# The rows of v by SBUF-to-SBUF DMA from a fourfold copy instead of by matmul, gamma in the collecting weights

## The reference, cut to what matters

```
q, k, v = split(layernorm(h) @ Wqkv.T + b)      # 16 heads of 16 channels
k = k / 4
retention = 1 - sigmoid(Lambda_raw)             # per head, 16 x 16
for every token t:
    hebbian[i, j] = v_t[i] * k_t[j]
    state = retention * state + Gamma * hebbian
    y_t[i] = sum_j (W_static[i, j] + state[i, j]) * q_t[j]
out = y @ out_w.T + out_b
```

## Time and profile before

| | us |
|---|---|
| median of 3 runs | 365.59 |
| lowest, highest | 363.73, 366.17 |
| span of the profiled execution | 360.0 |
| busy: DVE, PE, POOL, ACT | 302.0, 274.5, 207.5, 183.8 |
| first scan starts, last product ends | 45.72, 334.17 |

### The profile page before, as it was taken

The page is one execution under the profiler, slowest core; times in us unless marked ns, Lnnn a source line. Parts: engine busy times, 40 slices in busy tenths (PEclk is TensorE's granted clock), DMA queues, the critical chain, the costliest instruction groups (busy, mean ns, idle before and its releaser), DMA issues. The chain is left out here.

```text
span 360.0 us, 4155 instructions
## 1 busy us (share of the span) xinstructions
PE 274.5 (76%) x1214; PEld 141.5 (39%) x1214; DVE 302.0 (84%) x443; ACT 183.8 (51%) x336; POOL 207.5 (58%) x175
## 2 busy tenths in 40 slices
PE   5786899965979777965998498559978546747792
PEld 4674225531322353632333366223324213205581
DVE  0144098999999999999999999999999999999262
ACT  3236593455654704775768037576763168610152
POOL 5777676447873913747768317547876158970010
PEclk9899995996898799896999989887996956859899
DMA  6711200000010000000111000000210000001001
GB/s 168 251 46 49 75 7 2 3 0 0 13 50 26 0 3 1 0 0 29 36 50 33 4 1 0 0 31 0 74 44 3 0 0 0 0 15 46 0 2 58
DMA packets 10502, 10.07 MB, mean 28 GB/s; under 512 B 3344, under 2 KB 8944, under 8 KB 10480
## 3 DMA queue, kind: packets, MB, share of 16 engines
q1 hardware_dynamic: 9200, 7.70, 7.1%
q0 software_dynamic: 1280, 2.11, 2.1%
HBM read 4.95 MB, written 2.10 MB: 20 GB/s over the span
## 5 line engine op out<-in xcount | busy, mean ns | idle before, releaser
L380 POOL TENSOR_TENSOR uu<-vg,kk 128x512 f32<-128x512 f32 x128 | 160.1, 1275 | 99.7 <-ACT vg L566 93.7
L566 ACT ACTIVATE vg<-vr_ps,gam_sb 128x512 f32<-128x512 f32 x128 | 83.1, 687 | 20.3 <-PE vr_ps L882 12.6
L690 DVE TENSOR_TENSOR_SCAN zz<-r_ps,uu 128x512 f32<-128x512 f32 x64 | 77.2, 1214 | 10.3 <-POOL uu L380 10.3
L690 DVE TENSOR_TENSOR_SCAN zz<-r_ps,carry,uu 128x512 f32<-128x512 f32 x64 | 79.1, 1273 | 0.0
L711 DVE TENSOR_TENSOR zz<-zz,q_ps 128x1024 f32<-128x1024 f32 x64 | 76.4, 1196 | 0.0
L882 PE MATMUL vr_ps<-v_rows,selv 96*128 96x512 bf16 x100 | 40.5, 441 | 18.3 <-ACT vg L566 18.1
L896 PE MATMUL y_ps<-zz,sely 128*32 128x512 f32 x256 | 41.0, 717 | 15.2 <-DVE zz L711 15.2
L882 PEld LDWEIGHTS vr_ps<-v_rows,selv 96*128 96x128 bf16 x100 | 9.7, 102 | 55.8 <-ACT vg L566 38.9
L352 POOL TENSOR_TENSOR tok<-tok,bf 128x1024 f32<-128x1024 f32 x4 | 9.4, 2357 | 30.9 <-ACT tmp_b L482 29.3
L423 ACT ACTIVATE tok<-scr 128x512 f32<-128x512 f32 x16 | 9.5, 591 | 24.4 <-PE scr L812 17.5
L760 PE MATMUL scr<-wexp,emb_t 128*128 128x256 f32 x64 | 20.6, 479 | 1.0 <-ACT emb_t L415 1.0
(11 more groups left out here) (95 smaller groups left out, 413.3 us busy)
## 6 DMA issues: line engine op xcount, KB each, us to landing
v_rows<-v_part SPq DMA_DIRECT2D x84, 32.0 KB, 1.9
out_h<-tok SPq DMA_DIRECT2D x8, 256.0 KB, 2.2
wexp<-in_w_exp SPq DMA_DIRECT2D x1, 256.0 KB, 2.8
tok<-in_table,ids_sb POOLq DMA_INDIRECT x16, 2.8
wproj<-in_w_proj SPq DMA_DIRECT2D x1, 256.0 KB, 5.0
wv<-in_w_v SPq DMA_DIRECT2D x1, 256.0 KB, 4.8
wk<-in_w_k SPq DMA_DIRECT2D x1, 256.0 KB, 4.9
wq<-in_w_q SPq DMA_DIRECT2D x1, 256.0 KB, 5.3
```

The lines of the kernel that those rows point to most:

```text
L380: pool.tensor_tensor(uu[:, slot % NU, :], vg[:, slot % NVG, :], kk[:, c % 2, hg, :], ALU.mult).then_inc(s_u, 1)
L566: act.activation(vg[:, slot % NVG, :], vr_ps[:, slot % NVR, :], ACT.Copy, scale=gam_sb[:, n:n + 1]).then_inc(s_vg, 1)
L690: dve.tensor_tensor_scan(zz[:, g % NZ, :], r_ps[:, n:n + 1].to_broadcast([P, T]), uu[:, g % NU, :], start, ALU.mult, ALU.add).then_inc(s_s ...
```

## The change

- The splitting of v in three parts, `spread`, the PSUM buffers `vr_ps`, and ACT's copy with gamma go. v goes to SBUF once per head group, in fp32 (`v_sb`).
- `copy_v(c)` on SP, per chunk: for each head group four DMAs of 256 KB write `v_sb` to four places of an HBM tensor `v_far`. Then for each head group SP waits for these four and issues one DMA of 1 MB that reads them back as `v_four`. In it partition (h, j4, b) holds the rows a = 0..3, so each row of v lies on four partitions.
- `row(g)` on SP, per unit: one DMA of 256 KB from 32 partitions of `v_four` (each read four times, source step 0) straight into `vg`. POOL waits for it in place of ACT. There are eight `vg` buffers as before, and the DMA for unit g waits until POOL is done with unit g-8.
- `copy_v(c+1)` stands in SP's order behind `row` of unit 29 of chunk c, `store(c-1)` behind that of unit 31.
- gamma goes in the collecting weights: `gsel = sely * gamma`, two DVE instructions at the end of the prologue (`w_gam`); PE waits for them at slot 0.
- `wake` of the last chunk now uses `q_ps` and waits for all 64 products of DVE (`s_z`) instead of ACT's last `vg`. The calendars are otherwise unchanged but for the stages removed.

```diff
-NVR, NVG, NU, NZ = 2, 8, 8, 16
+NVG, NU, NZ = 8, 8, 16
+COPY_AT = 29
...
+            def copy_v(c):
+
+                for hg in range(HG):
+                    taken(sp, "v", c, hg)
+                    for j in range(NA):
+                        sp.dma_start(v_far[HG * c + hg, :, j], v_sb[:, hg, :]).then_inc(s_vfar[hg], 16)
+                for hg in range(HG):
+                    sp.wait_ge(s_vfar[hg], 16 * NA * (c + 1))
+                    if c >= 2:
+                        sp.wait_ge(s_u, UNITS * (c - 2) + HD * (hg + 1))
+                    sp.dma_start(v_four[:, c % 2, hg], v_far[HG * c + hg].rearrange("h j b a t -> (h j b) a t"))\
+                      .then_inc(s_v4[hg], 16)
+
+            def row(g):
+
+                c, n, hg, a, b = unit(g)
+                if n % HD == 0:
+                    sp.wait_ge(s_v4[hg], 16 * (c + 1))
+                if g >= NVG:
+                    sp.wait_ge(s_u, g - NVG + 1)
+                src = v_four[b::NB, c % 2, hg, a, :].rearrange("p (o t) -> p o t", o=1)
+                sp.dma_start(vg[:, g % NVG, :], src.to_broadcast([P // NB, NB, T])).then_inc(s_vrow[g % NVG], 16)
...
-            move_v(0)
-            for c in range(1, NC):
-                if c >= 2:
-                    store(c - 2)
-                move_v(c)
-            store(NC - 2)
+            copy_v(0)
+            for g in range(NC * UNITS):
+                row(g)
+                c, n, hg, a, b = unit(g)
+                if n == COPY_AT and c + 1 < NC:
+                    copy_v(c + 1)
+                if n == UNITS - 1 and c >= 1:
+                    store(c - 1)
             store(NC - 1)
...
-                    pool.wait_ge(s_vg, slot + 1)
+                    pool.wait_ge(s_vrow[slot % NVG], 16 * (slot // NVG + 1))
...
+            def v(c, hg):
+                bank = filled(act, "v", c, hg)
+                if c >= 1:
+                    act.wait_ge(s_vfar[hg], 16 * NA * c)
+                act.activation(v_sb[:, hg, :], scr[:, bank, :], ACT.Identity, bias=bv[:, hg:hg + 1])\
+                   .then_inc(s_free[bank], 1)
...
-                    act.wait_ge(s_vr, slot + 1)
-                    if slot >= NVG:
-                        act.wait_ge(s_u, slot - NVG + 1)
-                    n = slot % UNITS
-                    act.activation(vg[:, slot % NVG, :], vr_ps[:, slot % NVR, :], ACT.Copy,
-                                   scale=gam_sb[:, n:n + 1]).then_inc(s_vg, 1)
...
+            def w_gam(*_):
+                dve.wait_ge(s_w_unit, 48)
+                for hg in range(HG):
+                    units = slice(HD * hg, HD * (hg + 1))
+                    gam_of = gam_sb[:, units].rearrange("p (b a o) -> p b a o", a=NA, o=1)
+                    dve.tensor_tensor(gsel[:, units, :].rearrange("p (b a) m -> p b a m", a=NA),
+                                      sely[:].rearrange("p b (o m) -> p b o m", o=1).to_broadcast([P, NB, NA, 32]),
+                                      gam_of.to_broadcast([P, NB, NA, 32]), ALU.mult).then_inc(s_gsel, 1)
...
-                    bank = vr_ps[:, 0, :]
-                    pe.wait_ge(s_vg, NC * UNITS)
+                    bank = q_ps[:, 0, :]
+                    pe.wait_ge(s_z, NC * UNITS // 2)
...
-                    last = pe.matmul(y_ps[32 * a:32 * a + 32, :], sely[:, b, :], zz[:, (g + a) % NZ, :],
+                    last = pe.matmul(y_ps[32 * a:32 * a + 32, :], gsel[:, n + a, :], zz[:, (g + a) % NZ, :],
                                      start=False, stop=True, skip_group_check=True)
```

More of the change, by code:

```diff
@@ L124, in tower_kernel @@
     SLOTS = range(-1, (NC + 1) * UNITS)
-    uses = [key for slot in SLOTS for key in pe_at.get(slot, []) if not key[0].startswith(("v_less", "wake"))]
+    uses = [key for slot in SLOTS for key in pe_at.get(slot, []) if not key[0].startswith(("wake",))]
     use = {key: (n % 2, n // 2) for n, key in enumerate(uses)}
@@ L190, in tower_kernel @@
         q_sb = sb("q_sb", [P, HG, T])
-        v_part = [sb(f"v_part{p}", [P, HG, T], BF16) for p in range(PARTS)]
-        v_rows = sb("v_rows", [PARTS * 32, 2, HG, NA, T], BF16)
+        v_sb = sb("v_sb", [P, HG, T])
+        v_far = nc.dram_tensor("v_far", [NC * HG, P // HD, NA, NB, NA, T], F32).ap()
+        v_four = sb("v_four", [P, 2, HG, NA, T])
         y_t = sb("y_t", [P, HG, T])
@@ L231, in tower_kernel @@
         s_cast = sem("s_cast")
[L232 removed]
+        s_gsel = sem("s_gsel")
         s_sig = sem("s_sig")
@@ L861, in _ @@
             operand = {"expand": "base_t", "corr": "masked_t", "v": "xhat_t", "k": "xhat_t", "q": "xhat_t"}
-            def spread(g):
-                c, n, hg, a, b = unit(g)
-                direct = DIRECT if c else HD
-                if n == HD or n == direct:
-                    for p in range(PARTS):
-                        pe.wait_ge(s_vrows[p][hg], 16 * NA * moves(c, hg))
-                if g >= NVR:
-                    pe.wait_ge(s_vg, g - NVR + 1)
-                if n < direct:
-                    if n == 0:
-                        taken(pe, "v", c, 0)
-                    rows_a = slice(32 * a, 32 * a + 32)
-                    for p in range(PARTS):
-                        last = pe.matmul(vr_ps[:, g % NVR, :], selv[rows_a, b, :], v_part[p][rows_a, 0, :],
-                                         start=(p == 0), stop=(p == PARTS - 1))
-                    last.then_inc(s_vr, 1)
-                    return
-                pe.matmul(vr_ps[:, g % NVR, :], selv[0:PARTS * 32, b, :], v_rows[:, c % 2, hg, a, :],
-                          start=True, stop=True).then_inc(s_vr, 1)
             def collect(g):
@@ L960 @@
         "w_k": halves(w_qkv[DIM:2 * DIM].T),
-        "w_v": halves(w_qkv[2 * DIM:][rows].T),
+        "w_v": halves(w_qkv[2 * DIM:][v_rows].T),
         "b_q": b_qkv[:DIM].reshape(HG, P).T,
         "b_k": b_qkv[DIM:2 * DIM].reshape(HG, P).T,
-        "b_v": b_qkv[2 * DIM:][rows].reshape(HG, P).T,
+        "b_v": b_qkv[2 * DIM:][v_rows].reshape(HG, P).T,
         "w_o": halves(g["L0_attn_out_w"].T[rows]),
```

137 lines of the change are left out of this document (40 added, 97 removed).

## The result

| | before | after |
|---|---|---|
| median, lowest to highest | 364.71, 363.73 to 366.17 | 399.01, 396.82 to 402.07 |
| ratio, 95% interval | | 1.0948 [1.0877, 1.1019] |
| span of the profiled execution | 360.0 | 394.9 |

A forecast was written before the change was run, and what follows sets the result against it. The prediction took DVE to bound the 128 units. First scan +6.0, boundaries +4.5, end +6.0 and DVE's short instructions -11.5 made +5.0 us: a median of 370.6 us against 365.59, range 359 to 381 us.

The forecast's parts named there:

- The first scan: Start of the units: the chain of writes, read, row and multiplication delays the first scan from 45.72 to 51.8 us, +6.0 us.
- the price of a write: Copy of v to HBM: at 340 GB/s, 256 KB take 0.77 us of the DMA engines.
- SP's issuing: Copy of v before the first scan: issuing at 0.59 us a DMA is hidden below the transfers.
- v_four much beyond 15 us: Sign named in advance: the prediction is wrong if `v_four` lands much beyond 15 us after v.
- My upper bound: First scan: each of three hops 1.4 us slower, as the slowest `v_rows` landed, +10.3 us.
- The boundaries: Between chunks: `uu` of unit 30 comes 16 us after v; just in time once, 2.9 us late at unit 62; +4.5 us.
- The end: After the last product: wakes and collections now wait for it on PE, 8.0 us less a faster projection; +6.0 us taken.
- DVE's short instructions: In the units: POOL no longer waits for ACT, so stretched chain instructions give back 9.6 us and `carry` 2; -11.5 us.
- The rule of one POOL instruction per hit: In the units: a short DVE instruction waits until the POOL instruction in flight is done, about 1.24 us.
- the release by ACT: Cause given for POOL's bursts: it waited 93.7 us for ACT's `vg`, then caught up under DVE's layernorm chain.
- At nothing: Row transfers cost nothing: 0.77 us of the engines and 0.59 of SP against 1.74 us per unit; the traffic slows nobody.
- (D): Rival, chance 0.05: rows bind if a row's DMA takes over 1.74 us; at 2.2 us a row the kernel takes 424 us.

The follow-up runs named there:

- e13: Changed kernel, but each write of v to HBM goes in 32 blocks of 8 KB instead of 8 of 32 KB: 371.0 us, before beside it 362.9.
- e1: Changed kernel, but the last wakes use their own PSUM bank and wait for POOL's last `uu`, not DVE's last product: 423.1 us, before beside it 395.3.
- e17: e13 with the last wakes on their own bank behind POOL's last `uu` instead of DVE's last product: 392.2 us, before beside it 391.3.
- e0: The changed kernel run again, nothing altered: 399.8 us, before beside it 362.9, ratio 1.1013.
- e11: Changed kernel, but POOL makes each `uu` in two multiplications of 128x256 instead of one of 128x512: 411.1 us, before beside it 362.9.
- e18: Kernel before, but POOL may be three units ahead of DVE instead of eight: 379.9 us, before beside it 392.8, ratio 0.9691.
- e8: Changed kernel, but rows come straight from a doubled `v_sb`, 8 partitions read sixteen times, no HBM copy; wakes as in e1: 416.5 us, before beside it 395.3.
- e2: Changed kernel, but v is written to HBM once per head group and copied fourfold by four reads of 256 KB: 419.1 us, before beside it 395.3.

## Why the prediction was wrong

*The first scan, forecast +6.0, measured +14.8.* The step that failed is the price of a write: 0.77 us for 256 KB, from the window in which weights load. Those loads fill 128 partitions; the writes of v go to eight blocks, and eight engines carried them at 155 GB/s, 1.7 us each, 13.5 us for the eight. So the second read was out 14.3 us behind v at the first boundary and 15.8 in the prologue, not at 7.6. The price was taken by bytes, not by shape. The 1 MB reads were priced right: 3.1 us at 340 GB/s, found 332. Hung on to it: SP's issuing, costed at nothing, took 10.3 us for the eight writes in the prologue, so the first read went out 10.4 us behind v and not at 4.5:

```profile
34.98 10.33 SPq L288 DMA_DIRECT2D v_far<-v_sb  x8
...
45.35 5.39 SPq L293 DMA_DIRECT2D v_four<-v_far  x2
...
53.64 7.37 SPq L304 DMA_DIRECT2D vg<-v_four  x9
```

The first row, which waits for the first read, went out 18.7 us behind v (34.95 us); "v_four much beyond 15 us" was a sign of being wrong that the prediction had named. My upper bound (+10.3) stretched the landings and left the rate alone, so it did not cover the case either.

*The boundaries, forecast +4.5, measured +24.7.* The same chain, three times; the multiplication of unit 30 started 20.7 us behind v and not at 14.6. (The forecast's own parts, nothing, 2.9 and 2.9 us, add up to 5.8 and not to the 4.5 taken.) Unit 30 was to be just in time and came 6.4 us late, unit 62 was to be 2.9 late and came some 9 us late. With the writes at sixteen engines (e13) `uu` of these units started 15.1 to 15.5 us behind v, and the kernel took 371.0 us, +8.1 over before on its chip. Its parts are near the forecast ones, +8.2, +7.1, +6.2 and -12.9 us where +6.0, +4.5, +6.0 and -11.5 stood: the forecast was about that of a kernel whose writes use all engines. That the medians, 371.0 and 370.6 us, all but meet is luck, since before took 362.9 us there and not 365.6.

*The end, forecast +6.0, measured +8.5 in the profile,* 6 to 9 by e1, e17. The mechanism was right, and in e0 and e13 so was the size (+6.3 and +6.2). Timeline after, where the earlier trace rows had the collection alone:

```profile
360.67 5.91 PE L809 MATMUL q_ps<-idf 128*128 128x128 f32 x26 [9.64 <-DVE zz L692]
...
366.51 1.22 PE L844 MATMUL y_ps<-zz,gsel 128*32 128x512 f32 x8
...
367.66 1.61 PE L809 MATMUL q_ps<-idf 128*128 128x128 f32 x12
...
369.20 1.07 PE L844 MATMUL y_ps<-zz,gsel 128*32 128x512 f32 x8
...
370.33 0.60 ACT L446 ACTIVATE y_t<-y_ps 128x512 f32<-128x512 f32 x1 [32.84 <-PE y_ps L844]
...
371.61 1.03 PE L782 MATMUL scr<-wo,y_t 128*128 128x256 f32 x4
```

5.9, 1.2 and 1.6 us stood at 5.5, 1.1 and 1.4. The projection did start fast (1.03 us for four records), as counted on. In e0 the same 26 records took 4.56 us: most of the 2.2 us that the first profile has above e0 is in them and in the last layer, at a mean granted clock of 0.80 in this stretch against 0.87 in e0.

*DVE's short instructions, forecast -11.5, measured -13.1.* The sum came out about right by luck, since its parts did not: in the chain six hits went, not eleven (-5.2 us instead of -9.6), on `carry` six went (-5.7 us instead of -2). About 2 us are not traced to single instructions. The rule of one POOL instruction per hit was too narrow (e0, e11), and the reason given, the release by ACT, was a part at most: with POOL held at three units (e18), before gains as much (275.1 us of units against 275.3), its work for ACT unchanged.

The copies to `carry` and one line of the chain in the kernel after, against the earlier trace rows:

```profile
L680 DVE COPY carry<-zz x32: 135/142/850, 64.1 to 298.3; 128x2 f32<-128x2 f32 x32
```
```profile
L598 DVE SCALAR_TENSOR_TENSOR nr<-nr x16: 160/160/1324, 23.4 to 379.9; 128x2 f32<-128x2 f32 x16
```

*At nothing: the rows' transfers.* Right: 33 MB beside the scans left scan, product and multiplication at their length (1.27, 1.19 and 1.27 us; before 1.27, 1.20 and 1.27).

*The rivals.* None had it. (D) looked for a DMA slower than its bytes, but in the rows, and asked what one partition read many times costs; e8 shows a form that does it, through its eight partitions and not through the repeated reading. The Trainium skill, DMA: Bandwidth & Descriptors, section Anatomy of one DMA, gives its 2.0 us and 436 GB/s for DMAs issued from GpSimd; SP issues these. With the rule quoted above and half of that rate the eight writes would be an estimated 9.6 us; the 13.5 us found lie above that too.

## What to carry to other kernels

Price a DMA by its shape before its bytes: read the number in its outermost dimension on both sides, and where that is 8, look for 0.50 in the DMA share. Before replacing the engine that feeds a bound engine, try how far ahead the engine between them may run (here POOL, three units instead of eight): that gave as much in the units as the whole change (275.1 and 275.3 us). And what stands behind the last product on PE counts nearly in full: 8.7 us of such work cost 6.2 to 8.5.

## What the runs showed of the hardware

- A DMA whose outermost dimension counts 8 kept 0.47 to 0.50 of the engines busy in all three directions tried: SBUF to HBM at 155 GB/s (314 with 32 blocks), HBM to SBUF at 163 GB/s (e2), SBUF to SBUF at 113 GB/s (e8).
- A two-column copy on DVE waited up to 6.9 us, through eleven POOL instructions that ran without a pause (e11), 3.3 us in e0. The Trainium skill, SBUF — State Buffer, section SBUF: two separate sides, has the loser blocked for the other's whole instruction; the runs show that it can lose again to the next one. It isn't always so: around the first units of the kernel after POOL ran 17 multiplications in a row (59.20 to 80.05 us) and the four copies beside them took 0.14, 0.85, 0.39 and 0.82 us. What decides is open.
